# Decoder of three attention kinds on one core: the first transfers in another order and from two queues, the z weights in four pieces, constants made behind the first rows, and waits at their first use

## The chip, the cores and the metric

The kernel runs on one core of one Trainium2 chip. The metric is the time of one execution on the device in microseconds. Before the change it was 1535.69 us (median of 3 runs: 1531.51, 1535.69 and 1535.70). The profiled execution took 1535.67 us, of which 1533.9 us lie between its first and its last instruction. TensorE is called PE below, VectorE DVE, ScalarE ACT, GpSimd POOL, and SyncE, which here only issues transfers, SP.

## The reference: what is computed

32 independent samples of 128 rows by 128 features go through three layers, each with a residual and a layer norm. Cut to what matters:

```python
# self: q = k = raw heads of x (16 heads of 8 features), value = x itself
y = x.reshape(b, t, 16, 8).transpose(0, 2, 1, 3)
attn = softmax(einsum('bhtk,bhsk->bhts', y, y) / sqrt(8))
o = einsum('bhts,bsc->bhtc', attn, x)            # 16 x 128 columns
x = layernorm(x + o.transpose(0, 2, 1, 3).reshape(b, t, 2048) @ weight)   # 2048 x 128
# cross: q from x, k and v from ctx, 16 heads of 8, window |i - j| <= 64
x = layernorm(x + windowed_attention(x, ctx, Wq, bq, Wk, bk, Wv, bv, Wo, bo))
# local: two layers with token shift, l2-normed rotary q and k, 8 heads of 64,
# window of 64 back, then a gated MLP (gelu) of width 341
x = layernorm(x + local_layers(x, wqkv, q_scale, k_scale, wo, ln_g, ln_b, w1, b1, w2, b2))
```

## The kernel before

One sample is one tile of 128 partitions by 128 columns. The work on it is cut into stages: self attention (S), cross attention (C), and for each of two local layers an attention part (A, B) and an MLP part (M, N). The stages form a pipeline over samples: in iteration n, the self stage works on sample n - 1, the cross stage on sample n - 2, the local ones on samples n - 3 to n - 5. The first six iterations (n = 0 to 5) and the last five are written out, the rest is a loop; all call the same functions. Within an iteration each engine takes the stages' steps in the order of a string of letters (`ORDER_TENSOR` and its like, lines 66 to 73, unchanged here), and the engines meet through semaphores only. `again(v)` (line 108) is true for every sample but the first, so what stands under `if not again(v)` runs once.

The self stage avoids the large product at its end by moving it ahead. PE turns x (line 547), ACT copies the turned tile out as `kT` (732), and PE multiplies it with the 16 heads' weights `wz`, 512 columns at a time, into `z` (556, four products, each copied out by ACT at 737). POOL makes from `kT` the bf16 tiles `kb`, `qm` and `qmb` (1054 to 1060). Then come the scores for the row maxima (484), whose reduction is DVE's (853), the turned maxima (522), the scores again with the maxima subtracted (493 and 498), exp on ACT (726), and the weighted sum of `z` (569), which DVE adds up (890) and normalises.

What comes ahead of the first sample is what the change is about.

- SP issues all transfers of the kernel. It starts with the list `SETUP` (lines 374 to 379): the block of constants `con` (1288 columns: identity, shift, two masks, head patterns, cosines and sines), `wz`, four 128 x 128 weights, and four bias vectors, all counted on one semaphore, `loaded`. Then iteration 0 issues x of sample 0 (438). Then `prepare_local` issues the 40 transfers of the local layers' weights (431), and iteration 1 issues x of sample 1 and the context of sample 0 (443).
- PE, ACT, DVE and POOL each wait for all of `SETUP` (lines 455, 711, 826, 1022) before their first instruction that needs anything from memory.
- POOL then makes four bf16 constants (lines 1028 to 1031): `ident_b`, `hot_b`, and the masks `mask_n` and `mask_w`; each adds one to `prep_p`. Together with the memset of `half_neg` that makes 5, for which PE (457) and DVE (827) wait. Only after that does POOL copy x of sample 0 from `xin` to `x` (1051), for which the first instruction of PE waits (542).
- DVE fills six tiles by memset (820 to 825) and counts them on `prep_v`.
- In iteration 3 all engines run their `prepare_local`, which waits for the local weights.

The masks are used by the windowed cross stage (`mask_w`) and by the local attention (`mask_n`); `hot_b` and `ident_b` by all. Of `con`, the self stage uses the identity, the columns `C_HOT` and the columns `C_ROW`.

Of the kernel before, what the change touches and what calls it, by code (L numbers as in the profile page):

```python
# [51 lines left out]
C_SHIFT = C_ID + 128  # L52
C_MASKN = C_SHIFT + 128
C_BAND = C_MASKN + 128
C_HOT = C_BAND + 128
C_ROW = C_HOT + GH
C_OWN = C_ROW + GH
# [50 lines left out]
def again(v):  # L108

    return not (isinstance(v, int) and v == 0)  # L110
# [20 lines left out]
def decoder_kernel(nc, x, ctx_in, consts, w_heads, wqT, bq, wkT, bk, wvT, bv, woT, bo,  # L131
# [7 lines left out]
    with ExitStack() as ctx:  # L139
# [16 lines left out]
        half_neg = sb("half_neg", [128, H])  # L156
        wz = sb("wz", [128, H * 128])
# [18 lines left out]
        loaded = sem("attention_weights_loaded")  # L176
        local_loaded = sem("local_weights_loaded")
# [189 lines left out]
        def sample_rows(a, v):  # L367
# [7 lines left out]
            (con[:, :], consts), (wz[:, :], w_heads), (wq_s[:, :], wqT), (wk_s[:, :], wkT),  # L375
# [29 lines left out]
        N_PREP_P = 5  # L405
# [18 lines left out]
        @block.sync  # L424
        def _(sp):
            for tile, source in SETUP:
                sp.dma_start(tile, source).then_inc(loaded, 16)

            def prepare_local():
                for tile, source in SETUP_LOCAL:  # L430
                    sp.dma_start(tile, source).then_inc(local_loaded, 16)

            def iteration(i):
                v = at(i, 0)
                if v is not None:
                    if again(v):
                        sp.wait_ge(SELF.x_copied, v)
                    sp.dma_start(SELF.xin[:, :], sample_rows(x_rows, v)).then_inc(SELF.x_loaded, 16)
                v = at(i, 1)
                if v is not None:  # L440
                    if again(v):
                        sp.wait_ge(CROSS.cT_psum, v)
                    sp.dma_start(CROSS.cin[:, :], sample_rows(ctx_rows, v)).then_inc(CROSS.c_loaded, 16)
                v = at(i, 5)
                if v is not None:
                    sp.wait_ge(LOC[1].normed, v + STEP)
                    sp.dma_start(sample_rows(out_rows, v), LOC[1].out[:, 0, :]).then_inc(stored, 16)

            loop(nc.sync, iteration, prepare_local, 1)
            sp.wait_ge(stored, STEP * B)  # L450
# [3 lines left out]
        def _(pe):  # L454
            pe.wait_ge(loaded, LOADED)
            pe.wait_ge(prep_v, PREP_V_FIXED)
            pe.wait_ge(prep_p, N_PREP_P)
# [45 lines left out]
            def core16(s, v):  # L503

                pe.wait_ge(s.k_ready, v + STEP)
# [34 lines left out]
            def self_stage(v):  # L540
# [9 lines left out]
                for g in range(G):  # L550
                    bank = s.b0 if g % 2 else s.b1
                    if g == 0:
                        pe.wait_ge(s.xT_ready, v + STEP)
# [20 lines left out]
            def cross_stage(v):  # L574
                s = CROSS
                pe.wait_ge(s.c_loaded, v + STEP)
                pe.wait_ge(s.x_copied, v + STEP)
# [132 lines left out]
        def _(act):  # L710
            act.wait_ge(loaded, LOADED)
            act.wait_ge(prep_v, PREP_V_FIXED)

# [32 lines left out]
            def cross_stage(v):  # L746
# [3 lines left out]
                yield  # L750
                act.wait_ge(s.k_psum, v + STEP)
# [66 lines left out]
        def _(dve):  # L818
# [8 lines left out]
            dve.wait_ge(prep_p, N_PREP_P)  # L827
# [192 lines left out]
        def _(pool):  # L1020
            nc.gpsimd.memset(half_neg[:, :], -0.5).then_inc(prep_p, 1)
            pool.wait_ge(loaded, LOADED)
# [5 lines left out]
            copy(ident_b[:, :], ident).then_inc(prep_p, 1)  # L1028
            copy(hot_b[:, :, :], con[:, C_HOT:C_HOT + GH].unsqueeze(2).to_broadcast([128, GH, 128])).then_inc(prep_p, 1)
            for tile, at_ in ((mask_n, C_MASKN), (mask_w, C_BAND)):  # L1030
                copy(tile[:, :, :], con[:, at_:at_ + 128].unsqueeze(1).to_broadcast([128, GH, 128])).then_inc(prep_p, 1)
            pool.wait_ge(prep_v, PREP_V_FIXED)
# [13 lines left out]
            def self_stage(v):  # L1046
# [4 lines left out]
                copy(s.x[:, :], s.xin[:, :]).then_inc(s.x_copied, STEP)  # L1051
                yield
# [7 lines left out]
                copy(s.qmb[:, :, :], s.qm[:, :, :]).then_inc(s.low, STEP)  # L1060
                yield
# [114 lines left out]
```

## Time and profile before

| what | value |
|---|---|
| median of 3 runs | 1535.69 us |
| profiled execution, whole | 1535.67 us |
| its span, first to last instruction | 1533.9 us |
| PE busy | 1377.0 us (90%) |
| DVE busy | 1004.8 us (66%) |
| ACT busy | 952.5 us (62%) |
| POOL busy | 880.1 us (57%) |
| first instruction of PE (line 547) | 14.11 us after the start |
| mean granted clock of PE | 0.959 of full speed |

Busy shares are averages over the whole span. The change edits only what runs once ahead of the first sample and the place of some waits, so the rows to read are those of the first 45 us, in order of time, and then what the rest of the kernel still waits for from them.

### The profile page before, as it was taken

Reading aid. Unit: us, or ns where it says so; the run is one execution under the profiler, and the core shown is the slowest. Engines: PE = TensorE matmul, PEld = TensorE weight load, DVE = VectorE, ACT = ScalarE, POOL = GpSimd, SP = SyncE. Lnnn points to the kernel's source line nnn. Section 1 sums busy time; section 2 is a strip of 40 time slices with the busy share of each in tenths; the row PEclk is TensorE's granted clock in tenths of the full one; section 3 lists DMA queues with packets and bytes.
Section 4 is the critical chain, followed back from the end, with each engine's and each line's share of the span. In section 5 each row is a group of like instructions: output and inputs, shape, how many; then the busy total and the mean of one; then the engine's idle time right before and its main releaser. Section 6 shows DMA issues by size and latency. Waiting matters only on the chain. (4 is left out here: it accounts for less than half of the span.)

```text
span 1533.9 us, 38526 instructions
## 1 busy us (share of the span) xinstructions
PE 1377.0 (90%) x11993; PEld 938.6 (61%) x12088; DVE 1004.8 (66%) x2900; ACT 952.5 (62%) x2562; POOL 880.1 (57%) x1289
## 2 busy tenths in 40 slices
PE   4778999999999999999999999999999999998764
PEld 2445666666666666666666666666666666666553
DVE  1446677676677776766776767767767677677432
ACT  1234666676666766766667667666676676666642
POOL 1034556666665567666655676666555766665533
PEclk8678999999999999999999999999999999999975
DMA  4000000000000000000000000000000000000000
GB/s 146 11 5 4 5 7 5 5 2 5 5 5 5 5 3 5 2 5 5 5 5 5 3 5 2 5 5 5 5 5 3 5 2 5 5 4 4 3 3 4
DMA packets 21645, 12.47 MB, mean 8 GB/s; under 512 B 5816, under 2 KB 20834, under 8 KB 21474
## 3 DMA queue, kind: packets, MB, share of 16 engines
q1 hardware_dynamic: 21600, 11.95, 2.6%
q8 instruction: 21, 0.34, 0.1%
q14 instruction: 24, 0.18, 0.0%
HBM read 9.84 MB, written 2.10 MB: 8 GB/s over the span
## 5 line engine op out<-in xcount | busy, mean ns | idle before, releaser
L787 ACT ACTIVATE local_e<-local_ps,local_bias,local_rn 128x128 f32<-128x128 f32 x512 | 229.0, 491 | 18.1 <-DVE local_bias L961 18.0
L1109 POOL TENSOR_TENSOR local_rn<-local_sc,half_neg 128x8 f32<-128x8 f32 x128 | 212.7, 1662 | 7.5
L1127 POOL TENSOR_TENSOR local_e<-local_e,local_rd 128x512 f32<-128x512 f32 x128 | 133.0, 1040 | 134.5 <-DVE local_rd L965 133.3
L956 DVE TENSOR_REDUCE local_m<-local_ps 128x4 f32<-128x512 f32 x128 | 88.6, 692 | 104.6 <-PE local_ps L648 104.6
L569 PE MATMUL self_ps<-self_z,self_e 128*128 128x129 f32 x1024 | 147.5, 288 | 1.7 <-DVE self_y L890 0.8
L890 DVE SCALAR_TENSOR_TENSOR self_y<-self_ps,self_rd,self_y 128x128 f32<-128x128 f32 x448 | 133.2, 345 | 9.2
L569 PEld LDWEIGHTS self_ps<-self_z,self_e 128*128 128x128 f32 x1024 | 129.0, 197 | 15.8 <-issue 7.8
L1026 POOL TENSOR_SCALAR local_x<-local_out 128x256 f32<-128x256 f32 x32 | 12.9, 404 | 216.3 <-issue 216.3
L942 DVE TENSOR_TENSOR local_cosp<-local_ps,cos_t 128x512 f32<-128x512 f32 x128 | 87.2, 682 | 71.7 <-ACT local_sq L770 71.7
L556 PE MATMUL self_ps<-wz,self_kT 128*128 128x512 f32 x256 | 128.4, 626 | 1.8 <-ACT self_kT L732 1.8
L787 ACT ACTIVATION_READ_ACCUMULATOR local_e<-local_ps,local_bias,local_rn 128x1 f32 x512 | 122.4, 239 | 0.0
L770 ACT ACTIVATE local_sq<-local_ps 128x512 f32<-128x512 f32 x128 | 76.5, 598 | 59.4 <-PE local_ps L619 48.2
L737 ACT ACTIVATE self_z<-self_ps 128x512 f32<-128x512 f32 x128 | 76.5, 597 | 51.8 <-PE self_ps L556 51.4
L794 ACT ACTIVATE local_eT<-local_ps 128x512 f32<-128x512 f32 x128 | 75.4, 614 | 35.4 <-PE local_ps L656 35.2
L853 DVE TENSOR_REDUCE self_neg<-self_ps 128x4 bf16<-128x512 f32 x128 | 81.9, 682 | 23.1 <-PE self_ps L484 23.1
L853 DVE TENSOR_REDUCE cross_neg<-cross_ps 128x4 bf16<-128x512 f32 x128 | 82.2, 684 | 18.1 <-PE cross_ps L484 18.1
L656 PE MATMUL local_ps<-con,local_e 128*128 128x128 f32 x512 | 80.0, 281 | 15.0 <-POOL local_e L1127 14.9
L946 DVE TENSOR_TENSOR local_sinp<-local_ps,sin_t 128x512 f32<-128x512 f32 x128 | 86.9, 679 | 0.0
L951 DVE TENSOR_REDUCE local_ss<-local_sq 128x8 f32<-128x512 f32 x128 | 85.5, 668 | 0.0
L1113 POOL TENSOR_TENSOR local_cosp<-local_cosp,local_sinp 128x512 f32<-128x512 f32 x64 | 80.9, 1265 | 5.2 <-DVE local_sinp L946 5.2
L619 PE MATMUL local_ps<-wqkv_s,local_xT 128*128 128x512 f32 x128 | 70.9, 636 | 12.3 <-ACT local_xT L766 12.3
L1117 POOL TENSOR_TENSOR local_cosp<-local_cosp,local_sinp 128x512 f32<-128x512 f32 x64 | 81.2, 1268 | 1.0 <-DVE local_sinp L946 1.0
(173 smaller groups left out, 3436.1 us busy)
## 6 DMA issues: line engine op xcount, KB each, us to landing
self_xin<-x SPq DMA_DIRECT2D x32, 64.0 KB, 1.7
cross_cin<-ctx_in SPq DMA_DIRECT2D x32, 64.0 KB, 1.8
out<-local_out SPq DMA_DIRECT2D x32, 64.0 KB, 1.6
wqkv_s<-wqkv SPq DMA_DIRECT2D x2, 768.0 KB
wz<-w_heads SPq DMA_DIRECT2D x1, 1024.0 KB, 5.6
w_r<-w SPq DMA_DIRECT2D x2, 341.0 KB
con<-consts SPq DMA_DIRECT2D x1, 644.0 KB, 3.6
wo_s<-wo SPq DMA_DIRECT2D x2, 256.0 KB
```

Source lines behind the costliest of these rows:

```text
L556: nc.tensor.matmul(bank, s.kT[:, :], wz[:, 512 * g:512 * g + 512], start=True, stop=True)\
L569: last = nc.tensor.matmul(bank[:, 129 * j:129 * j + 129], s.e[:, h0 + j, :], s.z[:, h0 + j, :], start=True, stop=True)
L787: nc.scalar.activation(s.e[:, a, p, :], bank[:, 128 * p:128 * p + 128], ACT.Exp, bias=s.bias[:, a, p:p + 1], scale=s.rq[:, a, p:p + 1], ac ...
L853: nc.vector.tensor_reduce(s.neg[:, 32 * g:32 * g + GH], (s.odd if g % 2 else s.even).rearrange("p (j t) -> p j t", j=GH), AX.X, ALU.max, n ...
L890: nc.vector.scalar_tensor_tensor(out=s.y[:, h % 2, :], in0=bank[:, j, 0:128], scalar=s.rd[:, h:h + 1], in1=before, op0=ALU.mult, op1=ALU.a ...
L942: nc.vector.tensor_tensor(s.cosp[:, a, :, :], heads, cos_t[l][:, a, :].unsqueeze(1).to_broadcast([128, LH, LD]), ALU.mult)\
L946: nc.vector.tensor_tensor(s.sinp[:, a, :, :].rearrange("p h (u d) -> p h u d", u=2), halves[:, :, ::-1, :], sin_t[l][:, a, :].rearrange("p ...
L951: nc.vector.tensor_reduce(s.ss[:, LH * a:LH * a + LH], s.sq[:, a, :, :], AX.X, ALU.add)\
L956: nc.vector.tensor_reduce(s.m[:, a, :], bank.rearrange("p (c t) -> p c t", c=LH // 2), AX.X, ALU.max, negate=True)\
L1109: nc.gpsimd.tensor_tensor(s.rn[:, heads], s.sc[:, heads], half_neg[:, 0:LH], ALU.pow).then_inc(done, 8)
L1117: nc.gpsimd.tensor_tensor(s.cosp[:, 1, :, :], s.cosp[:, 1, :, :], s.sinp[:, 1, :, :], ALU.add).then_inc(s.q_roped, STEP)
L1127: nc.gpsimd.tensor_tensor(s.e[:, a, :, :], s.e[:, a, :, :], s.rd[:, a, :].unsqueeze(2).to_broadcast([128, LH // 2, 128]), ALU.mult)\
```

## The change

The transfers start in another order and from two engines. SP first issues x of sample 0, then only the first 136 columns of `con` (identity, `C_HOT` and `C_ROW`, which now lie together), counted on a semaphore of their own, and then the list `SETUP`, in which `con` means the other 1152 columns and `wz` no longer stands. ACT issues `wz` in four pieces of 512 columns, each with its own semaphore. The local weights are issued one iteration later: behind x of sample 1 and the context of sample 0.

The constants are made elsewhere in POOL's order: x of sample 0 is copied first, then `ident_b` and `hot_b` are made from the small piece of `con`, and the two masks after `qmb` of sample 0.

The waits stand at first use: PE starts on the small piece and waits for each piece of `wz` ahead of its product, for `ident_b` and `hot_b` ahead of the scores, for all of `SETUP` and for the masks in the first cross stage. ACT waits for `SETUP` ahead of the first bias of the cross stage. DVE's wait stays where it was, without the masks.

ACT also gets one more instruction, an exp of one column into a tile `warm`, behind its transfers.

```diff
-C_SHIFT = C_ID + 128
+C_HOT = C_ID + 128
+C_ROW = C_HOT + GH
+C_FIRST = C_ROW + GH
+C_SHIFT = C_FIRST
...
-            (con[:, :], consts), (wz[:, :], w_heads), (wq_s[:, :], wqT), (wk_s[:, :], wkT),
+            (con[:, C_FIRST:C_END], consts[:, C_FIRST:C_END]), (wq_s[:, :], wqT), (wk_s[:, :], wkT),
...
-        N_PREP_P = 5
+        N_PREP_P = 3
...
         @block.sync
         def _(sp):
-            for tile, source in SETUP:
-                sp.dma_start(tile, source).then_inc(loaded, 16)
+            def prepare():
+                for tile, source in SETUP:
+                    sp.dma_start(tile, source).then_inc(loaded, 16)
...
                     sp.dma_start(SELF.xin[:, :], sample_rows(x_rows, v)).then_inc(SELF.x_loaded, 16)
+                    if not again(v):
+                        sp.dma_start(con[:, 0:C_FIRST], consts[:, 0:C_FIRST]).then_inc(first_loaded, 16)
+                        prepare()
...
-            loop(nc.sync, iteration, prepare_local, 1)
+            loop(nc.sync, iteration, prepare_local, 2)
...
         @block.tensor
         def _(pe):
-            pe.wait_ge(loaded, LOADED)
+            pe.wait_ge(first_loaded, 16)
             pe.wait_ge(prep_v, PREP_V_FIXED)
-            pe.wait_ge(prep_p, N_PREP_P)
...
             def core16(s, v):
 
+                if not again(v):
+                    pe.wait_ge(made_first, 2)
+                    if s.windowed:
+                        pe.wait_ge(prep_p, N_PREP_P)
...
                     bank = s.b0 if g % 2 else s.b1
+                    if not again(v):
+                        pe.wait_ge(wz_loaded[g], 16)
...
                 pe.wait_ge(s.c_loaded, v + STEP)
+                if not again(v):
+                    pe.wait_ge(loaded, LOADED)
...
         @block.scalar
         def _(act):
-            act.wait_ge(loaded, LOADED)
+            for g in range(G):
+                act.dma_start(wz[:, 512 * g:512 * g + 512], w_heads[:, 512 * g:512 * g + 512]).then_inc(wz_loaded[g], 16)
             act.wait_ge(prep_v, PREP_V_FIXED)
+            nc.scalar.activation(warm[:, :], SELF.z[:, 0, 128:129], ACT.Exp)
...
                 yield
+                if not again(v):
+                    act.wait_ge(loaded, LOADED)
                 act.wait_ge(s.k_psum, v + STEP)
...
             dve.wait_ge(loaded, LOADED)
-            dve.wait_ge(prep_p, N_PREP_P)
+            dve.wait_ge(prep_p, 1)
...
             nc.gpsimd.memset(half_neg[:, :], -0.5).then_inc(prep_p, 1)
-            pool.wait_ge(loaded, LOADED)
...
-            copy(ident_b[:, :], ident).then_inc(prep_p, 1)
-            copy(hot_b[:, :, :], con[:, C_HOT:C_HOT + GH].unsqueeze(2).to_broadcast([128, GH, 128])).then_inc(prep_p, 1)
-            for tile, at_ in ((mask_n, C_MASKN), (mask_w, C_BAND)):
-                copy(tile[:, :, :], con[:, at_:at_ + 128].unsqueeze(1).to_broadcast([128, GH, 128])).then_inc(prep_p, 1)
-            pool.wait_ge(prep_v, PREP_V_FIXED)
+            def first_constants():
+
+                pool.wait_ge(first_loaded, 16)
+                copy(ident_b[:, :], ident).then_inc(made_first, 1)
+                copy(hot_b[:, :, :], con[:, C_HOT:C_HOT + GH].unsqueeze(2).to_broadcast([128, GH, 128])).then_inc(made_first, 1)
+
+            def other_constants():
+
+                pool.wait_ge(loaded, LOADED)
+                for tile, at_ in ((mask_n, C_MASKN), (mask_w, C_BAND)):
+                    copy(tile[:, :, :], con[:, at_:at_ + 128].unsqueeze(1).to_broadcast([128, GH, 128])).then_inc(prep_p, 1)
...
                 copy(s.x[:, :], s.xin[:, :]).then_inc(s.x_copied, STEP)
+                if not again(v):
+                    first_constants()
...
                 copy(s.qmb[:, :, :], s.qm[:, :, :]).then_inc(s.low, STEP)
+                if not again(v):
+                    other_constants()
```

The start of POOL's instructions in the kernel before, after its memsets (`self_xin` is the landing place of x; the waits are semaphores by name):

```order
8 L1026 TENSOR_SCALAR ident_b<-con 128x128 [waits attention_weights_loaded]
9 L1026 TENSOR_SCALAR hot_b<-con 128x512
10 L1026 TENSOR_SCALAR mask_n<-con 128x512
11 L1026 TENSOR_SCALAR mask_w<-con 128x512
12 L1026 TENSOR_SCALAR self_x<-self_xin 128x128 [waits self_x_loaded,prepared_by_vector]
13 L1026 TENSOR_SCALAR self_kb<-self_kT 128x128 [waits self_xT_ready]
14 L1056 TENSOR_TENSOR self_qm<-self_kT,con 128x512
15 L1026 TENSOR_SCALAR self_qmb<-self_qm 128x512 [waits self_q_wide]
```

And in the changed kernel, at the same place:

```order
8 L1045 TENSOR_SCALAR self_x<-self_xin 128x128 [waits self_x_loaded]
9 L1045 TENSOR_SCALAR ident_b<-con 128x128 [waits first_constants_loaded]
10 L1045 TENSOR_SCALAR hot_b<-con 128x512
11 L1045 TENSOR_SCALAR self_kb<-self_kT 128x128 [waits self_xT_ready]
12 L1083 TENSOR_TENSOR self_qm<-self_kT,con 128x512
13 L1045 TENSOR_SCALAR self_qmb<-self_qm 128x512 [waits self_q_wide]
14 L1045 TENSOR_SCALAR mask_n<-con 128x512 [waits attention_weights_loaded]
15 L1045 TENSOR_SCALAR mask_w<-con 128x512
```

The copy of x has moved from behind four constants to the front, and the masks behind `qmb`, together with the wait for all of `SETUP`.

PE's first instructions in the kernel before (`self_z_ready` and `self_max_done` stand for ACT's and DVE's answers):

```order
1 L547 MATMUL self_ps<-con,self_x 128x128 [waits prepared_by_pool,prepared_by_vector,self_x_copied,attention_weights_loaded]
2 L556 MATMUL self_ps<-wz,self_kT 128x512 [waits self_xT_ready]
3 L556 MATMUL self_ps<-wz,self_kT 128x512
4 L556 MATMUL self_ps<-wz,self_kT 128x512 [waits self_z_ready] x2
5 L484 MATMUL self_ps<-self_kb,self_qmb 128x128 [waits self_low,self_q_wide,self_k_ready,self_z_ready]
```

And in the changed kernel:

```order
1 L559 MATMUL self_ps<-con,self_x 128x128 [waits prepared_by_vector,self_x_copied,first_constants_loaded]
2 L570 MATMUL self_ps<-wz,self_kT 128x512 [waits self_xT_ready,self_weights0_loaded]
3 L570 MATMUL self_ps<-wz,self_kT 128x512 [waits self_weights1_loaded]
4 L570 MATMUL self_ps<-wz,self_kT 128x512 [waits self_z_ready,self_weights2_loaded]
5 L570 MATMUL self_ps<-wz,self_kT 128x512 [waits self_z_ready,self_weights3_loaded]
6 L492 MATMUL self_ps<-self_kb,self_qmb 128x128 [waits self_low,self_k_ready,self_q_wide,first_constants_made,self_z_ready]
```

The instructions are the same and in the same order; only their waits have changed.

ACT's first instructions in the changed kernel; before, the list began with the table load and `self_kT`:

```order
1 L728 DMA wz<-w_heads 128x512 x4
2 L730 ACT_TABLE_LOAD
3 L730 ACTIVATE warm<-self_z 128x1 [waits prepared_by_vector]
4 L750 ACTIVATE self_kT<-self_ps 128x128 [waits self_xT_psum]
5 L755 ACTIVATE self_z<-self_ps 128x4x128 [waits self_z_psum] x4
```

The table load has moved ahead of the wait for PE; the number of table loads in the whole program is the same.

## Rows read from the trace of the kernel before

**Rows 1.** Windows of the whole span (stretch, its length, busy time per engine, clock).
```profile
core 0: us, PE busy (x) PEld busy (x) DVE busy (x) ACT busy (x) POOL busy (x), PEclk, DMA share, GB/s
24.00:146.00 122.00, 96.83 (x618) 58.45 (x624) 56.38 (x163) 36.31 (x87) 29.59 (x51) 0.72 0.07 20
146.00:1446.00 1300.00, 1224.79 (x11111) 842.92 (x11197) 923.70 (x2662) 878.92 (x2379) 810.25 (x1179) 1.00 0.02 5
```
**Rows 2.** Timeline, 0 to 23 us (start, duration, engine, what; idle before and releaser).
```profile
0.74 0.38 SPq L427 DMA_DIRECT2D con<-consts  x1
5.58 0.43 SPq L438 DMA_DIRECT2D self_xin<-x  x1
11.66 0.30 POOL L1026 TENSOR_SCALAR ident_b<-con 128x128 bf16<-128x128 f32 x1 [10.82 <-DMA bo_r<-bo]
11.92 0.62 POOL L1026 TENSOR_SCALAR hot_b<-con 128x512 bf16<-128x512 f32 x1
13.67 0.30 POOL L1026 TENSOR_SCALAR self_x<-self_xin 128x128 f32<-128x128 f32 x1
14.11 0.45 PE L547 MATMUL self_ps<-con,self_x 128*128 128x128 f32 x1 [14.11 <-POOL self_x L1026]
14.66 1.28 ACT L732 ACT_TABLE_LOAD   x1 [14.66 <-PE self_ps L547]
15.96 0.28 ACT L732 ACTIVATE self_kT<-self_ps 128x128 f32<-128x128 f32 x1
16.38 5.27 PE L556 MATMUL self_ps<-wz,self_kT 128*128 128x512 f32 x8 [1.82 <-ACT self_kT L732]
17.36 0.34 PEld L556 LDWEIGHTS self_ps<-wz,self_kT 128*128 128x128 f32 x1 [0.52 <-issue]
19.23 0.52 PEld L556 LDWEIGHTS self_ps<-wz,self_kT 128*128 128x128 f32 x2 [0.68 <-issue]
20.52 0.30 PEld L556 LDWEIGHTS self_ps<-wz,self_kT 128*128 128x128 f32 x2 [0.78 <-issue]
22.40 0.40 PE L484 MATMUL self_ps<-self_kb,self_qmb 32*128 32x128 bf16 x8 [0.75 <-ACT self_z L737]
22.93 1.29 DVE L853 TENSOR_REDUCE self_neg<-self_ps 128x4 bf16<-128x512 f32 x2 [21.19 <-PE self_ps L484]
```
**Rows 3.** DMA issues by target, 0 to 50 us (size, median us from issue to landing).
```profile
wz<-w_heads SPq DMA_DIRECT2D x1, 1024.0 KB, 5.6
con<-consts SPq DMA_DIRECT2D x1, 644.0 KB, 3.6
wo_s<-woT SPq DMA_DIRECT2D x1, 64.0 KB, 4.5
bv_r<-bv SPq DMA_DIRECT2D x1, 64.0 KB, 3.9
bo_r<-bo SPq DMA_DIRECT2D x1, 64.0 KB, 6.5
```
**Rows 4.** The page's DMA issues over the whole span: x alone.
```profile
self_xin<-x SPq DMA_DIRECT2D x32, 64.0 KB, 1.7
```
**Rows 5.** Windows of the first transfers, columns as in Rows 1 (last: GB/s).
```profile
1.00:3.00 2.00, 0.00 (x0) 0.00 (x0) 0.62 (x4) 0.00 (x0) 0.00 (x0) 1.00 0.63 214
3.00:6.00 3.00, 0.00 (x0) 0.00 (x0) 0.00 (x0) 0.00 (x0) 0.00 (x0) 1.00 1.02 405
8.00:9.00 1.00, 0.00 (x0) 0.00 (x0) 0.00 (x0) 0.00 (x0) 0.00 (x0) 1.00 0.21 26
```
**Rows 6.** Timeline, 39 to 79 us: what the next samples and the local layers wait for.
```profile
39.66 0.43 SPq L443 DMA_DIRECT2D cross_cin<-ctx_in  x1
45.20 0.30 POOL L1026 TENSOR_SCALAR cross_x<-self_out 128x128 f32<-128x128 f32 x1 [0.23 <-DVE self_out L867]
78.25 2.46 PE L466 MATMUL local_ps<-lb_c,w_r 128*114 128x1 f32 x24
```
**Rows 7.** One line: the products with wz up to 60 us, either clock.
```profile
L556 PE MATMUL self_ps<-wz,self_kT x16: 592/620/1191, 16.4 to 53.1; 128*128 128x512 f32 x16
```

More of the change, by code:

```diff
@@ L51 @@
 C_ID = 0
-C_SHIFT = C_ID + 128
+C_HOT = C_ID + 128
+C_ROW = C_HOT + GH
+C_FIRST = C_ROW + GH
+C_SHIFT = C_FIRST
 C_MASKN = C_SHIFT + 128
 C_BAND = C_MASKN + 128
-C_HOT = C_BAND + 128
-C_ROW = C_HOT + GH
-C_OWN = C_ROW + GH
+C_OWN = C_BAND + 128
 C_COS = C_OWN + GH * 128
@@ L156, in decoder_kernel @@
         half_neg = sb("half_neg", [128, H])
+        warm = sb("warm", [128, 1])
         wz = sb("wz", [128, H * 128])
@@ L176, in decoder_kernel @@
         loaded = sem("attention_weights_loaded")
+        first_loaded = sem("first_constants_loaded")
+        wz_loaded = [sem(f"self_weights{g}_loaded") for g in range(G)]
+        made_first = sem("first_constants_made")
         local_loaded = sem("local_weights_loaded")
```

## Prediction

> **What bounds the kernel now.** I read the windows of the span first [rows 1]: between 146 and 1446 us PE is busy for 1224.8 of 1300 us at full granted clock. The loop is PE's, and the change edits nothing in it: the same instructions stand in the same order. So it can only win or lose in what runs once, and what it wins ahead of the first sample is won as a whole only if nothing later waits for an absolute time. The timeline of the first 23 us comes next [rows 2]. The first instruction of PE starts at 14.11 us, released by POOL's copy of x (13.67 to 13.97). That copy stands behind four constants, the first of which started at 11.66 when the last transfer of `SETUP`, bo_r, had landed. ACT then loads its table for 1.28 us while the turned tile waits for it. The transfers themselves come from the list of issues [rows 3, 4]. To see in them: x alone takes 1.7 us from issue to landing in the steady state, but it is issued as the eleventh transfer, at 5.58; and nothing that the self stage needs comes from the four bias vectors, for the last of which all engines wait.
>
> **The time from the start to the first product with wz.** Eleven issues of SP stand between 0.74 and 5.58, 0.48 us apart [rows 2].
>
> - x of sample 0 is now first: issued at 0.74, landed at 2.44 by the 1.7 us of [rows 4]. POOL copies it, 0.30 us, to about 2.8.
> - The small piece of con (68 KB) is issued at 1.22. From below it takes the 1.7 us of x, from above the 3.6 us of the whole con [rows 3], so it lands between 2.9 and 4.8. It is nearest in size to x; with ACT's pieces on the same engines I take 2.1, so 3.3. PE turns x at 3.4.
> - ACT issues four pieces. No row shows an issue on ACT; I price it like one of SP, 0.48. At nothing the lead would be 0.2 more (the turned tile then comes last), at twice that 1.9 less. ACT is free at 2.7. DVE's memsets are long done. The table load takes 1.28, the exp of one column at most the 0.28 of the copy of 128 columns; ACT is free at 4.2. The turned tile is there at 3.4 + 0.55 (14.11 to 14.66) = 3.95. So ACT copies at 4.2 and the first product with wz starts 0.42 later (15.96 to 16.38), at 4.6. Before it was 16.38: a lead of 11.8 us, of which 1.3 is the table load.
>
> If the small piece takes its upper end, PE turns x at 4.9 and the first product starts at 5.9: the lead is 10.5.
>
> The table load has a rule that speaks against so small a price. In [rows 2] the load ends at 15.94 and the copy behind it starts at 15.96, and it starts 0.10 after PE's end: no more than 1.3 us hangs on it. The Trainium skill (ScalarE: Activation LUTs, What ACT_TABLE_LOAD costs) adds a drain of about 1380 ns to the load on every switch to another set; by it ACT would be free at 5.6 and the lead 10.4; since DVE then waits less (below), the time would be 1525.3. The trace has no room for it at this first load, so the sum goes by the row.
>
> **The products with wz.** From the first one to the scores before: 16.38 to 22.40, 6.0 us. The fourth product starts 4.1 us after the first (20.52), so at 8.7. Will its weights be there? Until they are, both queues carry at most 1024 KB of wz and 964 KB of SP's (x, small piece, con, four weights). By [rows 5] 428 KB flow from 1 to 3 us and 405 KB per us from then on, so 2.0 MB have flowed at 6.9 us, and I leave a microsecond for the landing: 7.9. The slack is 0.8 us. The first three pieces have more: a quarter of the bytes at 3.2, needed at 4.6. So the wait for pieces costs nothing, and if the rate falls by a tenth or two, up to 1.
>
> PE's clock is no constant here. One load of weights takes 0.34 us at 17.36; at 20.52 two take 0.30 together [rows 2], and the product itself takes 592 ns at one level and 1191 at the other [rows 7]. So the clock rose between the second and the third product. If in the new kernel it does not, the last four passes take up to 2.4 us longer; if it rises earlier, about as many passes are faster by as much.
>
> **POOL and the constants.** ident_b and hot_b (0.30 and 0.62) follow the copy of x at 3.3 and are made at 4.2; the scores need them at 10.6. kb, qm and qmb follow the turned tile; before, all three fitted between its copy (done at 16.24) and the scores (22.40), and that distance is the same now. The masks (2 x 0.62) are behind the wait for SETUP and done by 13.4; queued behind them is only the root of the moments, more than 15 us later. This part is covered.
>
> **DVE's wait for SETUP.** This is the new last wait. DVE's first maximum started 0.53 us after the scores (22.40 to 22.93), so now at 11.15. But it still waits for bo_r, which is again the eleventh transfer, issued at 5.58. Its neighbour bv_r took 3.9 us and bo_r itself 6.5 [rows 3]: landed at 9.5 or at 12.1. The moving of wz to another queue does not help, since the slow stretch of the transfers (26 GB/s between 8 and 9 us, [rows 5]) comes when wz is long in (1.22 + 5.6 = 6.8). I take its own 6.5: DVE starts at 12.15, 1.0 us later than it could. Queued behind it are all four maxima, and PE waits for each pair. The whole stage before is shifted by 22.93 - 12.15 = 10.8 us. If bo_r is as quick as bv_r, by 11.8.
>
> **Does the shift last?** x of sample 1 and the context of sample 0 are now issued twelfth and thirteenth, at 6.1 and 6.6, instead of at 39.66 [rows 6], and are needed at 45.20 - 10.8 = 34.4. The local weights start 1 us later than before and take the 33 us of before (6.1 to 39.2), so the last is issued at about 40 and has landed some 5 us later. PE first uses them at 78.25 [rows 6], now at 67.4: 20 us of slack. x of sample 2 follows at 41, needed after 67 as well. I find no absolute time that comes first. Nothing in the loop differs.
>
> **Sum**, against the profiled execution (1535.67 us, of which 1533.9 span; the median of the runs shown is 1535.69, so no correction): lead 11.8, DVE's wait -1.0, the rest 0. 1535.67 - 10.8 = 1524.9 us.
>
> **The rivals.**
>
> *Late data.* The four pieces are served one behind the other, each with its own fixed part. From 1.7 us for 64 KB and 5.6 for 1024 KB, a piece of 256 KB takes 2.5, four in series 10.0: the last lands at 10.7, its product starts 2.1 late, DVE at 13.3, the gain is 9.7 and the time 1526.0. For it: two queues in use at once are in no row. Against it: con, wz and the four weights, issued 0.48 apart, landed at 4.3, 6.8 and (wo_s) 7.7, so their fixed parts overlapped. The Trainium skill (DMA: Bandwidth & Descriptors, Bandwidth) speaks for this rival: it advises batches of 1 MiB and more, since each transfer has a fixed part of about 2 us; by its fit four pieces in series would take 10.4. The same case holds a bo_r that lands later still, say at 15: 1528.
>
> *The clock.* The head start moves every later rise and fall of PE's clock against the work. Between 24 and 146 us the mean granted clock is 0.72 of full [rows 1]; with the two levels 0.5 and 1 that is 44% of 122 us at full clock, 54 us, and with PE busy for 96.8 of 122, 43 us of PE work at full clock. Each of these us takes two at the lower level. If an eighth of them falls, 5.4 us of the gain go and the time is 1530; it becomes slower than before from a quarter on (10.8 of 43), say 1538. For it: three runs of the same kernel spread by 4.2 us. Against: the order of work and its gaps are the same after the first maximum, so the same falls should come. It can as well give: 1521.
>
> *Hidden anyway.* If something later stands at an absolute time, the kernel stays at 1535.7. Only the local weights could do it, and they have 20 us.
>
> **How the numbers follow.** Forecast 0.68 (its own range 1522.5 to 1527); late data 0.15; clock that gives 0.06; clock that takes part 0.05; hidden 0.03; slower by the clock 0.03. The likeliest is 1524.9. The range that leaves out most of the last three cases and the outer end of the giving one is 1519 to 1529.5. A difference of 0.3% (4.6 us) is about what can be told from none: faster than 1531.1 are the first three and nearly all of the fourth, 0.93; same 0.04; slower 0.03.
>
> **What would show it right or wrong.** In the trace of the changed kernel: PE's first instruction between 3 and 5 us; ACT's table load ahead of it; the first product with wz at 4.6 and the fourth at 8.7, with no idle time that ends by a transfer; DVE's first maximum at about 12, released by bo_r rather than by PE; POOL's copy for the cross stage near 34.4 instead of 45.20; PE's first local product at 67.4 directly behind the work before it. The forecast is wrong if a piece of wz releases PE (late data), if the first local product waits for its weights, or if the stretch from there to the end is longer than before by more than a microsecond, with a lower mean clock up to 146 us.

## The result, and the profile after

The changed kernel took 1523.47 us (median of 5 runs, 1521.17 to 1524.53), the kernel before on the same chip 1531.51 us (5 runs, 1530.75 to 1535.70). The ratio is 0.9938 with a 95% interval of 0.9925 to 0.9952, that is 9.5 us less (7.4 to 11.5); the two medians themselves lie 8.0 us apart. The forecast of 1524.9 us, faster, holds. The profiled execution of the changed kernel took 1524.53 us, 11.1 us less than that of the kernel before, with a span of 1522.7 us.

The timeline of the changed kernel, 0 to 14 us, beside [rows 2] (start, duration, engine, what; idle before and releaser):

```profile
0.74 1.87 ACTq L728 DMA_DIRECT2D wz<-w_heads  x4
0.74 0.38 SPq L444 DMA_DIRECT2D self_xin<-x  x1
1.18 0.42 SPq L446 DMA_DIRECT2D con<-consts  x1
2.64 1.28 ACT L730 ACT_TABLE_LOAD   x1 [2.64 <-issue]
3.48 0.30 POOL L1045 TENSOR_SCALAR self_x<-self_xin 128x128 f32<-128x128 f32 x1 [2.63 <-DMA self_xin<-x]
4.92 0.45 PE L559 MATMUL self_ps<-con,self_x 128*128 128x128 f32 x1 [4.92 <-DMA con<-consts]
5.46 0.28 ACT L750 ACTIVATE self_kT<-self_ps 128x128 f32<-128x128 f32 x1 [1.33 <-PE self_ps L559]
5.88 6.52 PE L570 MATMUL self_ps<-wz,self_kT 128*128 128x512 f32 x8 [0.52 <-ACT self_kT L750]
6.80 0.43 SPq L433 DMA_DIRECT2D bo_r<-bo  x1
12.25 0.62 POOL L1045 TENSOR_SCALAR mask_n<-con 128x512 bf16<-128x512 f32 x1 [4.28 <-DMA bo_r<-bo]
13.15 0.40 PE L492 MATMUL self_ps<-self_kb,self_qmb 32*128 32x128 bf16 x8 [0.75 <-ACT self_z L755]
13.68 1.29 DVE L873 TENSOR_REDUCE self_neg<-self_ps 128x4 bf16<-128x512 f32 x2 [11.94 <-PE self_ps L492]
```

PE's first instruction starts at 4.92 instead of 14.11 us, and what releases it is the small piece of con, not the copy of x. The table load is off the path. The first product with wz starts at 5.88 instead of 16.38, and none of its pieces releases PE. DVE's first maximum is released by PE (13.15 + 0.53), not by bo_r, which has landed at 12.2.

The transfers of the changed kernel, 0 to 14 us, beside [rows 3] (size, median us from issue to landing), and the rate beside [rows 5]:

```profile
wz<-w_heads ACTq DMA_DIRECT2D x4, 256.0 KB, 5.7
con<-consts SPq DMA_DIRECT2D x1, 576.0 KB, 6.1
con<-consts SPq DMA_DIRECT2D x1, 68.0 KB, 3.6
bo_r<-bo SPq DMA_DIRECT2D x1, 64.0 KB, 5.4
```

```profile
1.00:3.00 2.00, 0.00 (x0) 0.00 (x0) 0.62 (x4) 0.36 (x1) 0.00 (x0) 1.00 0.41 137
3.00:6.00 3.00, 0.56 (x2) 0.33 (x2) 0.00 (x0) 1.40 (x3) 1.28 (x4) 1.00 0.92 267
```

The 5.7 us of a piece of 256 KB, as long as the whole 1024 KB took before, are a median: in order of issue the four took 3.0, 4.7, 6.7 and 7.0 us and landed at 3.7, 5.9, 8.4 and 9.2. The first lay ready 2 us before its product, but the weights of the third product were loaded from 8.74 on, only 0.3 us after its piece had landed. The rate between 3 and 6 us is 267 GB/s instead of 405. The small piece needs 3.6 us, the upper end of what was allowed for it.

Two later rows of the changed kernel, beside [rows 6]:

```profile
35.69 0.30 POOL L1045 TENSOR_SCALAR cross_x<-self_out 128x128 f32<-128x128 f32 x1 [0.23 <-DVE self_out L887]
68.34 0.86 PE L474 MATMUL local_ps<-lb_c,w_r 128*114 128x1 f32 x8
```

They are 9.5 and 9.9 us earlier than before. To follow the lead further I cut each execution at three events: DVE's first maximum, the issue of the first result's transfer, and that of the 28th. The way between the first two is called the fill, between the last two the loop, and the rest the drain.

| profiled execution | first maximum | fill | loop | drain | span |
|---|---|---|---|---|---|
| before | 22.93 | 192.68 | 1180.52 | 137.77 | 1533.9 |
| before, once more (below) | 24.19 | 187.82 | 1180.45 | 137.74 | 1530.2 |
| changed | 13.68 | 187.58 | 1181.74 | 139.70 | 1522.7 |
| changed, second | 14.32 | 187.32 | 1181.74 | 136.52 | 1519.9 |
| changed, third | 13.52 | 189.41 | 1183.26 | 138.71 | 1524.9 |

The lead at the first maximum is 9.25 us; the fill adds 5.1, the loop takes 1.2 and the drain 1.9 back. The experiments ask which of these belong to the change.

### The profile page after: what moved, and what is told of

The parts are those of the page before. It is cut to its first block and busy times, and to the rows that moved or that the text cites. A ratio compares the mean times of both kernels' runs of the same rounds, so it can differ in the third digit from the quotient of the medians.

```text
span 1522.7 us, 38533 instructions
## 1 busy us (share of the span) xinstructions
PE 1378.5 (91%) x11993; PEld 939.0 (62%) x12088; DVE 1004.0 (66%) x2900; ACT 952.8 (63%) x2563; POOL 879.9 (58%) x1289
## 5 line engine op out<-in xcount | busy, mean ns | idle before, releaser
L807 ACT ACTIVATION_READ_ACCUMULATOR local_e<-local_ps,local_bias,local_rn 128x1 f32 x512 | 137.6, 269 | 0.0
L635 PE MATMUL local_ps<-wqkv_s,local_xT 128*128 128x512 f32 x128 | 69.9, 628 | 12.2 <-ACT local_xT L786 12.2
```

What stands on the lines that cost most here:

```text
L807: nc.scalar.activation(s.e[:, a, p, :], bank[:, 128 * p:128 * p + 128], ACT.Exp, bias=s.bias[:, a, p:p + 1], scale=s.rq[:, a, p:p + 1], ac ...
```

## The experiments

Each was timed 5 times or more where a median is given, beside the kernel before on the same chip.

**The kernel before, once more.** No edit.

> The kernel before, profiled once more. In the profile that the prediction rests on, the way from DVE's first maximum (22.93) to the first transfer of a result (215.61) took 192.7 us, in all four profiles with the changed order 187.3 to 187.6. Theory A (chance of PE's clock in that one execution): here the way takes 187 to 189 us and the time is near 1531. Theory B (the kernel before has a slower fill of its own, for instance by its transfers at 39 us): 192 to 193 us again.

It took 1531.98 us, with a fill of 187.8: theory A. The windows of the stretch in which the 4.9 us lie, the kernel before in its first profile:

```profile
78.00:112.00 34.00, 25.88 (x154) 14.03 (x158) 17.63 (x50) 11.62 (x31) 13.10 (x20) 0.74 0.02 5
112.00:146.00 34.00, 29.61 (x200) 19.33 (x200) 18.24 (x55) 13.89 (x35) 12.81 (x24) 0.81 0.02 5
```

And in the second, from the same instruction (L466, here at 78.92) on:

```profile
79.00:113.00 34.00, 26.33 (x196) 14.86 (x197) 17.39 (x49) 14.63 (x40) 13.21 (x20) 0.82 0.02 5
113.00:147.00 34.00, 29.58 (x198) 19.25 (x199) 22.41 (x62) 13.01 (x30) 16.73 (x27) 0.88 0.02 5
```

The columns before the last two are what to compare: 0.74 and 0.81 of full clock against 0.82 and 0.88, from the same instruction on; in the same time the second profile gets through more of the work (111 instructions of DVE against 105). Over 68 us the 0.075 between the means are 5.1 us of full clock, an estimate that fits the 4.9 us. The first profile had drawn a slow fill. So the 5.1 us which the fill seems to give are no part of the change. Nor is the way from the first product with wz to the scores a constant of the kernel: 6.0 us in the first profile, and here 16.27 to 23.66, 7.4:

```profile
16.27 6.64 PE L556 MATMUL self_ps<-wz,self_kT 128*128 128x512 f32 x8 [1.82 <-ACT self_kT L732]
23.66 0.40 PE L484 MATMUL self_ps<-self_kb,self_qmb 32*128 32x128 bf16 x8 [0.75 <-ACT self_z L737]
```

Between the two profiles with like fills (187.8 and 187.6), 24.19 to 13.68 is a lead of 10.5 at the first maximum; over all profiles of the two kernels it is 8.6 to 10.7.

**The changed kernel, twice more.** No edit.

> The changed kernel as it is, to stand beside the others. Theory 1 (the start alone): PE's first instruction is released by the small piece of con at 4.8 to 5.0 us, the median lies 9 to 11 us under the kernel before, 1521 to 1524.5. Theory 2 (the granted clock in the first 150 us decides several us): PE's start and DVE's first maximum stand where they stood, but the way from the first maximum (13.7) to the first transfer of a result (201.3 in the trace of the changed kernel, a way of 187.6) differs by 2 us or more from that.

> The changed kernel once more, to stand beside the others on this chip: 1521 to 1524.

Medians 1521.71 us (5 runs; before 1531.09; ratio 0.9938, 0.9924 to 0.9952) and 1521.80 us (5 runs; before 1531.54; ratio 0.9932, 0.9917 to 0.9947). The three comparisons give 9.5, 9.5 and 10.4 us by their ratios (8.0, 9.4 and 9.7 between the medians), the same within their intervals. PE's first instruction was not at 4.8 to 5.0, though: in both profiles the small piece took 4.6 us and PE started at 5.87. Nor did the fill differ by the 2 us of theory 2: it was 187.3 in one, and 189.4 in the other. The 5 us by which the fill can differ stand between the two profiles of the kernel before; they move single executions and do not make the difference of the medians.

**All waits of PE back.**

```diff
+            pe.wait_ge(loaded, LOADED)
             pe.wait_ge(first_loaded, 16)
```

> PE alone waits again for all of SETUP before its first instruction; transfers, pieces, table load and POOL's order stay as changed. Theory 1: SETUP has landed at 12.2, so PE starts at 12.3 instead of 4.9, 7.4 later; the table is loaded by then, so the scores follow at 12.3 + 8.2 = 20.5. Time 7 us over the changed kernel, about 1531. Rival (the order of the transfers and the table load carry the gain, not the waits): within 2 us of the changed kernel.

1527.31 us (8 runs), 5.6 over the changed kernel on the same chip (1521.71). The timeline of this kernel, PE alone:

```profile
10.51 0.45 PE L560 MATMUL self_ps<-con,self_x 128*128 128x128 f32 x1 [10.51 <-DMA bo_r<-bo]
11.48 6.40 PE L571 MATMUL self_ps<-wz,self_kT 128*128 128x512 f32 x8 [0.52 <-ACT self_kT L751]
```

bo_r had landed at 10.5, earlier than the 12.2 of the expectation, which explains why the loss is 5.6 and not 7. From its PE start of 10.51 and that of the second profile of the changed kernel, 5.87, the loss should be 4.6; from the first one, 4.92, it should be 5.6. So theory 1, and about three fifths of the gain is lost when PE waits for all of SETUP.

**x of sample 0 behind SETUP again.**

```diff
-                    sp.dma_start(SELF.xin[:, :], sample_rows(x_rows, v)).then_inc(SELF.x_loaded, 16)
                     if not again(v):
                         sp.dma_start(con[:, 0:C_FIRST], consts[:, 0:C_FIRST]).then_inc(first_loaded, 16)
                         prepare()
+                    sp.dma_start(SELF.xin[:, :], sample_rows(x_rows, v)).then_inc(SELF.x_loaded, 16)
```

> x of sample 0 is issued behind SETUP again (eleventh), all waits and pieces as changed. Theory 1 (order and waits are worth something only together): x lands at 9.5 to 12, POOL's copy and PE's first instruction follow at 10 to 12.5, 5 to 7 us later than in the changed kernel; the time is 5 to 7 us over it, like with all waits of PE back. Rival (the waits alone carry the gain): within 2 us of the changed kernel.

1526.85 us (6 runs), 5.1 over the changed kernel on the same chip (1521.80). PE is now released by POOL's copy of x, which waited for its transfer:

```profile
10.53 0.45 PE L559 MATMUL self_ps<-con,self_x 128*128 128x128 f32 x1 [10.53 <-POOL self_x L1045]
```

With all waits at first use, the late x costs as much as PE's wait did. Either edit taken out of the changed kernel loses the same 5 to 6 us, so this part of the gain needs both. A kernel with both taken out was not run; that it would start hardly later than these two (10.51 and 10.53) is read from the rows.

**Without the exp of one column.**

```diff
-            nc.scalar.activation(warm[:, :], SELF.z[:, 0, 128:129], ACT.Exp)
```

> Without the exp of one column. The table load falls behind PE's first product, on the path. Theory 1: 1.3 us later at every point, +1.3 us over the changed kernel. By the page's drain (ScalarE: Activation LUTs of the Trainium skill) it would be 2.7. Rival (hidden by PE's low clock or by transfers): no difference at DVE's first maximum.

1522.93 us (5 runs), 1.2 over the changed kernel on the same chip. The timeline of this kernel shows the load between PE and the copy:

```profile
4.81 0.45 PE L559 MATMUL self_ps<-con,self_x 128*128 128x128 f32 x1 [4.81 <-DMA con<-consts]
5.37 1.28 ACT L749 ACT_TABLE_LOAD   x1 [5.37 <-PE self_ps L559]
6.66 0.28 ACT L749 ACTIVATE self_kT<-self_ps 128x128 f32<-128x128 f32 x1
7.08 6.29 PE L570 MATMUL self_ps<-wz,self_kT 128*128 128x512 f32 x8 [1.82 <-ACT self_kT L749]
```

From PE's start to the first product with wz are 2.27 us instead of 0.96: 1.3 us, the load alone. The 2.7 us that the Trainium skill (ScalarE: Activation LUTs, What ACT_TABLE_LOAD costs) gives for a switch with its drain do not appear at this first load. The 1.2 us of the medians is within the spread of the runs; the row carries the verdict.

**PE later by a known length.** POOL writes ten tiles of zeros ahead of its copy of x; the output is not touched.

```diff
                 pool.wait_ge(s.x_loaded, v + STEP)
+                if not again(v):
+                    for _ in range(10):
+                        nc.gpsimd.memset(pad[:, _, :], 0.0)
```

> POOL writes ten tiles of 128 x 512 zeros (into a tile that nothing reads) ahead of the copy of x of sample 0, all else as in the changed kernel. PE starts later by the length of these writes less the 1.4 us by which the copy of x is early; ten writes of 0.4 to 0.6 us make PE start 3 to 5 us later. Theory 1 (a start is worth its own length): the median rises over the changed kernel by what DVE's first maximum moves, within 1 us. Rival (the fill has slack, or the clock eats or gives it): the median moves by less than half of that.

The writes took 4.68 us, PE started at 8.41 and the first maximum at 17.04, 2.7 to 3.5 us later than in the three profiles of the changed kernel. The median was 1528.23 us (12 runs; ratio to before 0.9969, 0.9956 to 0.9983), so 0.31% or 4.7 us behind the changed kernel (ratio 0.9938). This is 1 to 2 us more than the start moved, just outside what theory 1 said; both intervals are 2 us wide to each side, so they can't tell 3.5 from 4.7. In the profile the fill is 187.5 as elsewhere, but the loop is 1182.7. The rival, less than half of the delay, is out: a start is worth about its own length, and the fill shows no slack.

**The small piece first on ACT.**

```diff
-                        sp.dma_start(con[:, 0:C_FIRST], consts[:, 0:C_FIRST]).then_inc(first_loaded, 16)
...
+            act.dma_start(con[:, 0:C_FIRST], consts[:, 0:C_FIRST]).then_inc(first_loaded, 16)
             for g in range(G):
                 act.dma_start(wz[:, 512 * g:512 * g + 512], w_heads[:, 512 * g:512 * g + 512]).then_inc(wz_loaded[g], 16)
```

> The small piece of con is issued first on ACT, beside x on SP, and not second on SP. Theory 1: both land by 3.5 us, PE starts at 3.6 and ACT, with five issues and the table load, is free at 4.6, so the copy kT starts at 4.7 instead of 5.46 and the time falls by 0.8 us. If the small piece is late because of its short rows or its place among the big ones and not because of its place on SP, PE starts at 4.6 to 5.0 as before and nothing is won.

1522.11 us (5 runs), no gain over 1521.71 on the same chip. The small piece took 2.2 us and PE started at 3.39, as hoped. But the next wait was right behind, in a row that no profile had shown before:

```profile
3.39 0.45 PE L558 MATMUL self_ps<-con,self_x 128*128 128x128 f32 x1 [3.39 <-POOL self_x L1045]
6.86 6.16 PE L569 MATMUL self_ps<-wz,self_kT 128*128 128x512 f32 x8 [3.02 <-DMA wz<-w_heads]
```

The first piece of wz, issued at 1.2, took 5.6 us and landed at 6.8; in all three profiles of the changed kernel it took 3.0 and landed at 3.7. The rate between 3 and 6 us was no lower (282 GB/s against 267). So the start is bound by the transfers, and by whose bytes come first as well as by the rate. The next two runs ask what sets the rate.

**All pieces on SP.**

```diff
                         sp.dma_start(con[:, 0:C_FIRST], consts[:, 0:C_FIRST]).then_inc(first_loaded, 16)
+                        for g in range(G):
+                            sp.dma_start(wz[:, 512 * g:512 * g + 512], w_heads[:, 512 * g:512 * g + 512]).then_inc(wz_loaded[g], 16)
...
-            for g in range(G):
-                act.dma_start(wz[:, 512 * g:512 * g + 512], w_heads[:, 512 * g:512 * g + 512]).then_inc(wz_loaded[g], 16)
```

> The four pieces of wz are issued on SP behind the small piece of con, ACT issues nothing. In the trace of the changed kernel the transfers ran at 267 GB/s between 3 and 6 us, in the one before at 405. Theory P (the pieces' rows of 2 KB cost the rate): the rate stays near 270, and SETUP lands at 12 to 13. Theory Q (two queues on the same 16 engines disturb each other): the rate goes back to about 400, and the small piece lands by 3 us since nothing competes. In either case PE's first instruction comes earlier than 4.9, because wz stands behind the small piece; ACT's table load ends at 2.1, so kT at about 4 and the first product with wz at 4.5 if its piece is there: 1.0 to 1.5 us faster than the changed kernel. If the wait moves to DVE for SETUP, 0 to 0.5.

**wz in one piece on ACT.**

```diff
-            for g in range(G):
-                act.dma_start(wz[:, 512 * g:512 * g + 512], w_heads[:, 512 * g:512 * g + 512]).then_inc(wz_loaded[g], 16)
+            act.dma_start(wz[:, :], w_heads).then_inc(wz_loaded[0], 16)
```

> wz is one transfer of 1024 KB on ACT, with rows of 8 KB, and all four products wait for it. Theory P (rows of 2 KB cost the rate): the rate between 3 and 6 us is near 400 GB/s, wz lands at about 6.3 and the first product starts then, 0 to 0.5 us later than in the changed kernel, since the copy kT is there at 5.7; the time stays within 1 us. Theory Q (two queues): the rate stays near 270, wz lands at 8 or later, and the time rises by 2 us.

The windows of the kernel with all pieces on SP, columns as in [rows 5]:

```profile
3.00:6.00 3.00, 1.50 (x3) 0.68 (x3) 0.00 (x0) 0.28 (x1) 1.93 (x4) 1.00 0.85 281
```

And of the kernel with one piece on ACT:

```profile
3.00:6.00 3.00, 0.00 (x0) 0.00 (x0) 0.00 (x0) 0.00 (x0) 0.30 (x1) 1.00 0.99 400
```

As theory P said, the rate stays at 281 GB/s with four pieces though one queue issues everything, and is 400 with one piece though two queues do. The number of queues does not set the rate. But these runs do not show that the rows of 2 KB do, since the one piece also replaces four transfers. And the pieces do not hold the rate at 270 to 280: in the run with x of sample 0 behind SETUP, with the same four pieces, it was 327 from 3 to 6 us:

```profile
3.00:6.00 3.00, 0.00 (x0) 0.00 (x0) 0.00 (x0) 1.13 (x2) 0.00 (x0) 1.00 0.98 327
```

In the three profiles of the changed kernel 382 to 386 GB/s flowed from 6 to 8 us, while the last two pieces were still on their way. What the mix of transfers does to the rate stays open. The number of queues does change who gets it. The pieces on SP took 4.2 us in the median instead of 5.7 and the small piece 2.7 instead of 3.6. The first rows of that kernel:

```profile
0.73 1.28 ACT L730 ACT_TABLE_LOAD   x1 [0.73 <-PEq L1198]
3.97 0.45 PE L561 MATMUL self_ps<-con,self_x 128*128 128x128 f32 x1 [3.97 <-DMA con<-consts]
4.95 6.48 PE L572 MATMUL self_ps<-wz,self_kT 128*128 128x512 f32 x8 [0.53 <-DMA wz<-w_heads]
12.71 1.29 DVE L873 TENSOR_REDUCE self_neg<-self_ps 128x4 bf16<-128x512 f32 x2 [10.97 <-PE self_ps L494]
```

It took 1519.96 us (6 runs, 1518.20 to 1520.85; ratio to before 0.9907, 0.9884 to 0.9929). Its first maximum is at 12.71, 1.0 us ahead of the changed kernel's. It has the lowest median of all kernels that ran and beats the kernel before; against the changed kernel, which did not run beside it, it is 1.8 to 3.5 us lower in the medians, but the intervals of the ratios overlap. The kernel with one piece took 1522.50 us (6 runs; ratio 0.9924, 0.9902 to 0.9947): its small piece took 4.9 us and wz 5.1, PE started at 6.13, and all four products then found their weights. All of wz was in at 5.8 instead of 9.2, but the small piece was late although 400 GB/s flowed from 3 to 6 us, so a low rate is not what makes it late.

**The small piece on ACT, all else on SP.** Also, DVE waits for SETUP only in the cross stage.

```diff
-                        sp.dma_start(con[:, 0:C_FIRST], consts[:, 0:C_FIRST]).then_inc(first_loaded, 16)
+                        for g in range(G):
+                            sp.dma_start(wz[:, 512 * g:512 * g + 512], w_heads[:, 512 * g:512 * g + 512]).then_inc(wz_loaded[g], 16)
...
+            act.dma_start(con[:, 0:C_FIRST], consts[:, 0:C_FIRST]).then_inc(first_loaded, 16)
...
-            dve.wait_ge(loaded, LOADED)
-            dve.wait_ge(prep_p, 1)
```

> The small piece of con goes first on ACT, x first on SP, behind it the four pieces of wz and the rest on SP; DVE waits for SETUP only in its first cross stage. PE starts at 3.1 to 3.6 (small piece 2.2 us after 0.74), kT is copied at 4.1, and the first piece of wz, issued at 1.2, lands at 4.5 if it takes the 3.3 us that it took with all of wz on SP: first product at 4.5, DVE's first maximum at 12.2. So 0.4 us under the kernel with all of wz on SP, 3 us under the changed kernel. If two queues at the start slow the first piece, the product waits for it until 5 or later and nothing is won over that kernel.

1521.83 us (6 runs; ratio 0.9936, 0.9921 to 0.9950), nothing won over the 1521.80 of the changed kernel on the same chip. PE started at 3.39, but the first product at 4.95, released by its piece. The first maximum came at 12.82, yet the loop took 1183.92 us, 3.3 more than with the pieces on SP.

**PE kept busy with zeros.** As the last kernel, with 18 products of zeros ahead of x and 7 ahead of the first product with wz.

```diff
+            pe.wait_ge(prep_v, PREP_V_FIXED)
+            keep_busy(18)
             pe.wait_ge(first_loaded, 16)
...
                     if g == 0:
+                        if not again(v):
+                            keep_busy(7)
                         pe.wait_ge(s.xT_ready, v + STEP)
```

> As the kernel with the small piece first on ACT, and PE multiplies tiles of zeros (18 products of 128 columns ahead of x, 7 between the turned x and the first product with wz) into a bank that is overwritten later. If the low clock in the products with wz is a consequence of PE's idleness before them, they run at the higher clock: from the first product to the scores 5 to 6 us instead of 7.1, and 1 to 2 us less time. If the clock does not rise, or the zeros push PE's own work back, the time is equal or up to 0.5 us longer.

1521.55 us (6 runs, 1518.71 to 1525.65; ratio 0.9929, 0.9914 to 0.9945): no difference from the last one. The profile shows both effects:

```profile
1.81 2.10 PE L467 MATMUL cross_ps<-self_neg 128*128 128x128 bf16 x18 [1.81 <-DVE local_xT L852]
4.88 0.93 PE L467 MATMUL cross_ps<-self_neg 128*128 128x128 bf16 x7 [0.75 <-DMA wz<-w_heads]
5.60 5.37 PE L578 MATMUL self_ps<-wz,self_kT 128*128 128x512 f32 x8
11.72 0.40 PE L498 MATMUL self_ps<-self_kb,self_qmb 32*128 32x128 bf16 x8 [0.75 <-ACT self_z L762]
```

From the first product to the scores are 6.1 us against 7.4 in the last kernel. But the seven zeros stand behind the wait for the piece and push the product from 4.95 to 5.60, and the third profile of the changed kernel has the same 6.1 us (6.84 to 12.99) without any zeros. Whether the zeros raise the clock is not shown by one profile; the 0.6 us won at the first maximum were not seen in the median.

## Why the prediction was right, and where it was not

**The mechanism was right.** The gain is a head start ahead of the first sample. It is about as large in the medians (8.0 to 9.7 us) as at the first maximum (8.6 to 10.7). From PE's first local product to the end are 1455.7 and 1451.3 us in the two profiles before, and 1454.4, 1451.2 and 1456.0 in the three of the changed kernel, so no loss on the way can be told, though the loop alone is 1.2 to 2.8 us longer. The local weights do not bound anything (PE's first local product at 68.34, where 67.4 was forecast), and the rival "hidden anyway" is out. Putting back PE's wait or x's place costs what the start loses.

**The lead at the first product, 11.8 forecast, 10.5 measured.** The step that was mis-sized is the small piece of con: 2.1 us taken between bounds of 1.7 and 3.6, and it took 3.6, and 4.6 in two further profiles. I had given it the 1.7 us of a lone transfer of its size and 0.4 for ACT's pieces beside it. That their place beside it matters is shown: behind it on its own queue they leave it 2.7 us, and it takes 2.2 when it is first on ACT. The table load was priced rightly at 1.3, and ACT's four issues at 0.47 each, as on SP.

**DVE's wait, -1.0 forecast, 0 measured.** bo_r landed at 12.2 as forecast, which was luck: it was issued at 6.80 and not at 5.58, since SP's issues did not stay 0.48 apart, and took 5.4 us and not 6.5; in the two other profiles it landed by 10.3 and 10.7. The scores came at 13.15 instead of 10.6, so PE released DVE. The reason is the way from the first product with wz to the scores. I took 6.0 us from the profile; it is 6.0 to 7.4 over the profiles, 7.3 in the changed one. The eight passes of these products took 592 to 1191 ns each, with a median of 658 in the first profile before and of 1061 in the changed one. The column of the granted clock reads 1.00 in this stretch in both, so that the clock is what differs is read from the passes alone. I had named this risk and then priced it at zero.

**The shift at the first maximum, 10.8 forecast, 9.25 measured**: 11.8 - 10.5 = 1.3 from the small piece, 1.3 from the clock (7.27 instead of 6.02), less the 1.0 of DVE's wait, make the 1.6 that are missing.

**The time, 1524.9 forecast, 1523.5 measured.** That it is so near is in part luck. It was summed on a profiled execution of 1535.67 us, 4 us above the median of the kernel before (1531.51, and 1531.1 to 1533.0 in the later comparisons), because its fill had run at the low clock. Without that, the same sum would have said 1520.7, and the smaller lead 1522.3. Two errors of opposite sign, 4 and 1.6 us, partly cancel. The rival "the clock" was real, but as a draw of single executions of both kernels, not as something that the head start does.

**Late data.** The rival in which pieces wait one for another did not come as a wait, but luck had a part in that. The prediction carried the 405 GB/s of [rows 5] over to the new mix and had all pieces in by 7.9; 267 GB/s flowed between 3 and 6 us, and the last two landed at 8.4 and 9.2. Had PE started when forecast, it would have wanted the third at 7.5 (4.6, and the 2.85 from 16.38 to 19.23 in [rows 2]) and waited 0.9 us for it, an estimate from these rows. The rival's own number was too high as well: four pieces in series were to take 10.0 us, and the last was in 8.5 after the first issue. The Trainium skill (DMA: Bandwidth & Descriptors, Bandwidth) says that small transfers lose rate. The runs agree so far that four pieces brought less than one (265 to 282 GB/s between 3 and 6 us, and 327 with x late, against 400); whether by their number or their rows of 2 KB is not shown.

**Where the gain lies.** PE's wait together with x at the front is 5 to 6 us. With PE's wait back, the first product with wz still starts at 11.48 instead of 16.38. Of these 4.9 us the table load is 1.3, the earlier landing of SETUP 1.1 (10.5 against 11.66), and 2.5 are the four constants and the copy of x that no longer follow that landing (11.66 to 14.11). Only the table load was tried apart; the other two are read from the rows.

## What to carry to other kernels

Order the first transfers by their first use and let each engine wait for its own piece at that use; here 5 to 6 us of the gain needed both. A small transfer that gates the start takes the time of the traffic beside it, not its own (3.3 to 4.9 us here with bulk on the other queue), so try it ahead of the bulk on the same queue (2.7). Then look at what is needed next: with the small piece in at 2.9, the first piece of wz was the wait. Before summing on a profile, check whether that execution lies at the median, and look at the granted clock of its fill: a difference of 4 us was in one draw.

## What the runs showed of the hardware that was not expected

- Rate by the mix: with wz in four pieces (128 rows of 2 KB each) and x in front, 265 to 282 GB/s flowed between 3 and 6 us, with one queue or two; with wz in one transfer (rows of 8 KB) 400 to 405. With the same pieces it was 327 there when x came later, and 382 to 386 from 6 to 8 us with x in front, so the length of the rows alone does not set it.
- Pieces of one size on one queue do not take the same time: 3.0, 4.7, 6.7 and 7.0 us from issue to landing, within 0.1 us in three profiles.
- The iteration of the loop has a length that is constant to 0.03 us within an execution but differs between them: 43.73 us in both profiles of the kernel before and in three others, 43.77 in two profiles of the changed kernel and 43.83 in the third, 43.86 in the last two kernels. From the first result to the 28th this makes 1180.45 to 1183.92 us, 3.5 us between the extremes. Between 146 and 1446 us the granted clock is 1.00 both before ([rows 1]) and in the changed kernel. The cause was not tried and stays open; in the profiles of the last two kernels it took more than the 1 us back that they had won at their first maximum.
- The first maximum and the drain move by 1 to 3 us in otherwise equal executions: the drain took 136.5 to 139.7 us in three profiles of the same kernel.
